# The first stage of a fused cross-attention kernel in a new order: loads in near and far parts, mask sum on ScalarE, all media turned first, mixing and splits interleaved with keys and maxima

## The reference

```
# layer 0, per batch
q  = layernorm(x) @ Wq / 8;   k, v = split(media @ Wkv)        # 16 heads of 64
sim = where(mask, q @ k.T, lowest float)                       # (16, 256, 1601)
x  = x + tanh(attn_gate) * (softmax(sim) @ v) @ Wo
x  = x + tanh(ff_gate) * gelu(layernorm(x) @ W1) @ W2
# layer 1, per batch
mem = media @ W_mem.T;  ctx = softmax(x @ mem.T / 16) @ mem
x = x + sigmoid([x, ctx] @ W_gate.T + b_gate) * ctx;  out = rmsnorm(x) * norm_w
```

## Time and profile before

| what | us |
|---|---|
| device time, median of 3 runs | 901.36 (900.8 to 902.85) |
| span of the profiled execution, first to last instruction | 897.9 |
| busy in that span: PE, DVE, ACT, POOL | 849.0, 592.1, 460.7, 397.7 |

### The profile page before, as it was taken

How to read it: one execution, slowest core, us unless ns; L and a number is a source line. 1 busy time by engine, 2 the same in 40 slices (tenths; PEclk the granted TensorE clock), 3 DMA queues, 4 the chain that set the end, 5 groups by cost and what they waited for, 6 DMA issues and landing times.

```text
span 897.9 us, 18267 instructions
## 1 busy us (share of the span) xinstructions
PE 849.0 (95%) x7811; PEld 709.2 (79%) x7811; DVE 592.1 (66%) x955; ACT 460.7 (51%) x724; POOL 397.7 (44%) x180
## 2 busy tenths in 40 slices
PE   3789999999999999999999999999999999999987
PEld 2478878888878888888888888888887778888775
DVE  6666688867848888677588886756787612043363
ACT  3465555656635556575356665735554441234352
POOL 2155555555645556566256565663566550000000
PEclk9699999999999999999999999999999999999999
DMA  9000001000000010000000000000001500001100
GB/s 273 24 1 1 1 1 38 1 2 1 2 1 1 1 38 2 1 1 2 1 2 1 1 1 2 1 2 1 1 2 39 166 1 0 1 1 37 38 24 23
DMA packets 19842, 16.67 MB, mean 19 GB/s; under 512 B 930, under 2 KB 18739, under 8 KB 19763
## 3 DMA queue, kind: packets, MB, share of 16 engines
q1 hardware_dynamic: 19474, 15.25, 5.8%
q10 hardware_dynamic: 288, 0.27, 0.1%
HBM read 14.46 MB, written 1.05 MB: 17 GB/s over the span
## 4 chain that ended last, share of the span: by engine, by line
PE 78%; DVE 12%; ACT 5%; issue 2%; POOL 1%; DMA 1%; POOLq 0%; DVEq 0%
PE psum L1239 21%; PE psum L1253 16%; PE psum L338 14%; PE psum L1204 6%; PE psum L1162 3%; PE psum L1268 3%; PE psum L1017 3%; PE psum L1031 3%; PE psum L1104 3%; DVE mx L871 2%; DVE k_lo L860 2%; DVE ot L901 1%; PE psum L1259 1%; POOL acc L435 1%; ACT k_hi L591 1%
## 5 line engine op out<-in xcount | busy, mean ns | idle before, releaser
L435 POOL TENSOR_TENSOR acc<-acc,ring 128x1024 f32<-128x1024 f32 x128 | 306.6, 2396 | 18.7 <-POOL acc L435 0.5
L871 DVE TENSOR_REDUCE mx<-psum 128x2 f32<-128x800 f32 (+2 forms) x256 | 245.5, 990 | 88.4 <-PE psum L1204 80.6
L614 ACT ACTIVATE ring<-psum 128x1024 f32<-128x1024 f32 x192 | 196.8, 1026 | 67.6 <-PE psum L1239 61.0
L430 POOL TENSOR_TENSOR acc<-ring 128x1024 f32<-128x1024 f32 x32 | 76.6, 2394 | 283.9 <-ACT ring L614 283.9
L1253 PE MATMUL psum<-ring,v 128*64 128x256 f32 (+1 forms) x1664 | 186.7, 381 | 1.7
L1253 PEld LDWEIGHTS psum<-ring,v 128*64 128x64 f32 (+1 forms) x1664 | 116.7, 137 | 61.0 <-DVE k_lo L860 3.8
L1239 PE MATMUL psum<-nm,maskrow 64*128 64x256 f32 (+1 forms) x832 | 124.1, 294 | 0.6 <-ACT ring L614 0.6
L1239 PE MATMUL psum<-q_hi,k_hi 64*128 64x256 f32 (+1 forms) x832 | 117.3, 278 | 0.0
L1239 PE MATMUL psum<-q_lo,k_hi 64*128 64x256 f32 (+1 forms) x832 | 117.0, 277 | 0.0
L1239 PE MATMUL psum<-q_hi,k_lo 64*128 64x256 f32 (+1 forms) x832 | 117.0, 277 | 0.0
L608 ACT COPY od<-psum 128x512 f32<-128x512 f32 x32 | 18.8, 587 | 172.3 <-PE psum L1259 172.3
(11 more groups left out here) (151 smaller groups left out, 1371.2 us busy)
## 6 DMA issues: line engine op xcount, KB each, us to landing
nat<-in_ctx_dram SPq DMA_DIRECT2D x8, 768.0 KB
w<-in_L_xattn_W_dram SPq DMA_DIRECT2D x2, 1024.0 KB, 8.1
ring<-in_L_xattn_Wkv_dram SPq DMA_DIRECT2D x2, 512.0 KB, 10.1
wq<-in_L_xattn_Wq_dram SPq DMA_DIRECT2D x1, 1024.0 KB, 10.2
wo<-in_L_xattn_Wo_dram SPq DMA_DIRECT2D x1, 1024.0 KB, 11.1
out_dram<-t_res SPq DMA_DIRECT2D x8, 128.0 KB, 1.8
mask<-in_mask_BxS_bk_dram SPq DMA_DIRECT2D x4, 200.1 KB, 6.9
xs<-in_x_dram SPq DMA_DIRECT2D x3, 256.0 KB, 6.7
```

Source lines behind the costliest of these rows:

```text
L430: nc.gpsimd.tensor_tensor(acc[:, :, :, :], ring[:, 0, :, :, :], ring[:, 1, :, :, :], ALU.add)\
L435: nc.gpsimd.tensor_tensor(acc[:, :, :, :], acc[:, :, :, :], ring[:, g, :, :, :], ALU.add)\
L614: nc.scalar.activation(ring[:, g, :, :, :], score_set[m % 2].rearrange("p (h i q) -> p h i q", h=2, i=2), ACT.Exp).then_inc(S["p_ready"], 1)
L871: nc.vector.tensor_reduce(mx[:, t, :, c], pair[:, :, 0:min(c1, KEYS) - c0], axis=AX.X, op=ALU.max).then_inc(S["m_max"], 1)
```

## The change

It does these things. The media of batch 0 load in two parts (six tiles, then the rest), and Wk, Wq and Wv in a near part (the first 256 columns, `NEAR`) and a far part. The mask sum of every batch is an ACT activation with accumulation instead of a DVE reduction; DVE's scalars (B) wait for it, and the inverted mask (J) is an item of its own, placed later. The masked copy T reads the mask itself instead of the inverted mask. In the first stage Z comes ahead of all T, four units of T ahead of W, and G.4 (ACT's q_hi too) ahead of the splits; the low part of q is a new item Q. The items P and K of one chunk alternate, and K.8.2 and the splits alternate with the first maxima. I.1.0, I.1.1, V.4.5 and V.4.6 move back, V.4.6 behind the first scores. POOL now makes the high part of Wv as well, splits the near parts when they are there, and the far parts after the last mt_lo; the first exponential waits for the far parts.

```
...
+FULL_EXTRAS = {2: "G.3 Q.3", 3: "T.1.0 T.1.1 T.1.2", 4: "T.1.3 T.1.4", 5: "W.1", 6: "G.4 Q.4", 7: "G.5 Q.5", 9: "O.0 H.0 G.6 Q.6"}
+COLUMN_EXTRAS = {2: "B.1 J.1", 3: "X.1", 4: "Z.1 C.1 Y.1.0 Y.1.1 Y.1.2 Y.1.3", 5: "P.1.0 P.1.1 P.1.2 P.1.3", 7: "I.1.0 I.1.1"}
...
     ahead = [i for i in body if i[1] >= AHEAD[i[0]]]
-    early = items("""X.1 B.1 I.1.0 T.1.0 T.1.1 Z.1 T.1.2 W.1 T.1.3 T.1.4 C.1 Y.1.0 P.1.0 Y.1.1 P.1.1 Y.1.2 P.1.2 Y.1.3 P.1.3 G.4
-                     K.8.0 K.8.1 K.8.2 K.8.3 M.8.0 M.8.1 L.8.0 M.8.2 M.8.3 L.8.1 L.8.2 L.8.3 I.1.1 V.4.0 M.8.4 V.4.1 M.8.5 V.4.2
-                     M.8.6 V.4.3 M.8.7 V.4.4 N.8 V.4.5 V.4.6 K.9.0 L.9.0 K.9.1 L.9.1 R.8 K.9.2 L.9.2 K.9.3 L.9.3""")
-    behind_scores = items("G.5")
+    early = items("""X.1 B.1 Z.1 T.1.0 T.1.1 T.1.2 T.1.3 W.1 T.1.4 G.4 J.1 C.1 Y.1.0 Y.1.1 P.1.0 K.8.0 Y.1.2 P.1.1 K.8.1 Y.1.3 P.1.2
+                     K.8.2 P.1.3 L.8.0 M.8.0 M.8.1 K.8.3 L.8.1 Q.4 M.8.2 M.8.3 I.1.0 V.4.0 V.4.1 L.8.2 M.8.4 M.8.5 V.4.2 V.4.3
+                     L.8.3 M.8.6 M.8.7 I.1.1 V.4.4 K.9.0 K.9.1 N.8 R.8 L.9.0 L.9.1 K.9.2 L.9.2 K.9.3 L.9.3 V.4.5 S.8.0""")
+    behind_scores = items("V.4.6 G.5 Q.5")
...
     TUNITS = -(-KT // TURN)
+    NEAR = 4 * HD
...
 
-    FIRST_KEYS = (3, 1, 0, 2)
+    FIRST_BANKS = dict(zip(items("T.1.0 T.1.1 T.1.2 T.1.3 W.1 T.1.4 G.4 K.8.0 K.8.1 K.8.2 K.8.3 V.4.5"),
+                           (0, 1, 2, 3, 1, 0, 2, 3, 0, 1, 3, 0)))
 
     def bank_of(order, item):
-        return FIRST_KEYS[item[2]] if order is FIRST and item[:2] == ("K", PAIRS) else BANK[item]
+        return FIRST_BANKS.get(item, BANK[item]) if order is FIRST else BANK[item]
...
             sp.dma_start(mask8[:, 0, :], media_mask[0:1, :].broadcast_to([P, KEYS])).then_inc(S["mask0_in"], 16)
-            sp.dma_start(nat0[:, 0:KT - 1, :], media_full[0, :, :, :]).then_inc(S["media_in"], 16)
+            sp.dma_start(nat0[:, 0:2 * TURN, :], media_full[0, :, 0:2 * TURN, :]).then_inc(S["media0_in"], 16)
+            sp.dma_start(nat0[:, 2 * TURN:KT - 1, :], media_full[0, :, 2 * TURN:KT - 1, :]).then_inc(S["media_in"], 16)
             sp.dma_start(nat0[0:TAIL, KT - 1, :], media_tail[0, :, :]).then_inc(S["media_in"], 16)
-            sp.dma_start(raw_kv[:, 0:INNER], Wkv[:, 0:INNER]).then_inc(S["wk_in"], 16)
-            sp.dma_start(wq[:, :, :], Wq.rearrange("(t p) n -> p t n", p=P)).then_inc(S["wq_in"], 16)
-            sp.dma_start(raw_kv[:, INNER:2 * INNER], Wkv[:, INNER:2 * INNER]).then_inc(S["wv_in"], 16)
+            wq_v = Wq.rearrange("(t p) n -> p t n", p=P)
+            for part, w in enumerate((slice(0, NEAR), slice(NEAR, INNER))):
+                sp.dma_start(raw_kv[:, w], Wkv[:, w]).then_inc(S["wk_in", part], 16)
+                sp.dma_start(wq[:, :, w], wq_v[:, :, w]).then_inc(S["wq_in", part], 16)
+                sp.dma_start(raw_kv[:, INNER:2 * INNER][:, w], Wkv[:, INNER:2 * INNER][:, w]).then_inc(S["wv_in", part], 16)
...
             reciprocal_root(0, "rstd_ready")
-            pool.wait_ge(S["wk_in"], 16)
-            nc.gpsimd.tensor_copy(wk_hi[:, :], raw_kv[:, 0:INNER]).then_inc(S["kv_hi"], 1)
-            for i, (lo, hi) in enumerate(((wk_lo, wk_hi), (wv_lo, wv_hi))):
-                pool.wait_ge(S["kv_hi"], i + 1)
-                nc.gpsimd.tensor_tensor(lo[:, :], raw_kv[:, i * INNER:(i + 1) * INNER], hi[:, :].bitcast(F32),
-                                        ALU.subtract).then_inc(S["kv_split"], 1)
+            for n, w in enumerate((slice(0, NEAR), slice(NEAR, INNER))):
+                if n:
+                    pool.wait_ge(S["mt_lo"], NCH)
+                for i, (name, lo, hi) in enumerate((("wk_in", wk_lo, wk_hi), ("wv_in", wv_lo, wv_hi))):
+                    raw = raw_kv[:, i * INNER:(i + 1) * INNER]
+                    pool.wait_ge(S[name, n], 16)
+                    nc.gpsimd.tensor_copy(hi[:, w], raw[:, w]).then_inc(S["kv_hi"], 1)
+                    pool.wait_ge(S["kv_hi"], 2 * n + i + 1)
+                    nc.gpsimd.tensor_tensor(lo[:, w], raw[:, w], hi[:, w].bitcast(F32), ALU.subtract)\
+                        .then_inc(S["kv_split"], 1)
...
                     kind, n = item[0], item[1]
-                    if order is FIRST and item == ("I", 1, 1):
-                        act.wait_ge(S["wv_in"], 16)
-                        nc.scalar.copy(wv_hi[:, :], raw_kv[:, INNER:2 * INNER]).then_inc(S["kv_hi"], 1)
                     if kind in USES_BANK:
                         bank = aux[bank_of(order, item)]
-                    if kind == "P":
+                    if kind == "B":
+                        if order is FIRST:
+                            act.wait_ge(S["mask0_in"], 16)
+                        upto(act, "qs_ready", b, n)
+                        nc.scalar.activation(unread[:, :], mask8[:, b + 1, :], ACT.Copy, accum_out=msum[:, 0:1])\
+                            .then_inc(S["mask_summed"], 1)
+                    elif kind == "P":
...
                         upto(act, "s_full", b, 2 * (m + 1))
+                        if order is FIRST and item == ("S", PAIRS, 0):
+                            act.wait_ge(S["kv_split"], 4)
...
 
-                        if order is FIRST:
-                            dve.wait_ge(S["mask0_in"], 16)
-                        step(nc.vector.reduce_sum(msum[:, 0:1], mask8[:, b + 1, :], axis=AX.X))
+                        upto(dve, "mask_summed", b, n + 1)
                         nc.vector.tensor_scalar(msum[:, 1:2], msum[:, 0:1], 0.5, None, ALU.is_le)
                         step(nc.vector.tensor_scalar(msum[:, 2:3], msum[:, 0:1], 1.0, None, ALU.max))
                         nc.vector.tensor_scalar(qs[:, :], msum[:, 1:2], -Q_SCALE, Q_SCALE, ALU.mult, ALU.add)\
                             .then_inc(S["qs_ready"], 1)
                         step(nc.vector.reciprocal(msum[:, 3:4], msum[:, 2:3]))
+                    elif kind == "J":
                         nc.vector.tensor_scalar(inv8[:, :], mask8[:, b + 1, :], msum[:, 1:2], 0.5, ALU.max, ALU.is_lt)\
                             .then_inc(S["inv_ready"], 1)
                     elif kind == "T":
                         c0, c1 = turned(item[2])
                         upto(dve, "t_full", b, n * TUNITS + item[2] + 1)
-                        upto(dve, "inv_ready", b, n + 1)
-                        nc.vector.scalar_tensor_tensor(mt[:, c0:c1], inv8[:, c0:c1], 0.5, bank[:, 0:c1 - c0],
-                                                       ALU.is_lt, ALU.mult).then_inc(S["mt_in"], 1)
+                        nc.vector.scalar_tensor_tensor(mt[:, c0:c1], mask8[:, b + 1, c0:c1], msum[:, 1:2],
+                                                       bank[:, 0:c1 - c0], ALU.max, ALU.mult).then_inc(S["mt_in"], 1)
                     elif kind == "C":
                         upto(dve, "part_in", b, (n + 1) * TUNITS)
                         step(nc.vector.reduce_sum(msum[:, 4:5], part[:, :], axis=AX.X))
+                        upto(dve, "inv_ready", b, n + 1)
...
                                                 ALU.subtract).then_inc(S["mt_lo"], 1)
-                    elif kind == "G":
+                    elif kind == "Q":
                         upto(dve, "q_hi", b, n + 1)
+                        bank = aux[bank_of(order, ("G", n))]
...
                     if kind == "T":
-                        if item[2] == 0:
+                        if order is FIRST and item[2] == 0:
+                            pe.wait_ge(S["media0_in"], 16)
+                        elif item[2] == 2 * (order is FIRST):
...
                     elif kind == "G":
-                        if order is FIRST and n == PAIRS // 2:
-                            pe.wait_ge(S["wq_in"], 16)
+                        if order is FIRST and n < PAIRS // 2 + 2:
+                            pe.wait_ge(S["wq_in", n - PAIRS // 2], 16)
...
                             pe.wait_ge(S["kv_split"], 1)
+                        if order is FIRST and item == ("K", PAIRS + 2, 0):
+                            pe.wait_ge(S["kv_split"], 4)
...
```

More of the change, by code:

```diff
@@ L34 @@
          "F": PAIRS, "V": PAIRS // 2, "G": PAIRS // 2, "O": 1, "H": 1, "T": 1, "B": 1, "C": 1, "Y": 1, "P": 1, "X": 1, "Z": 1,
-         "W": 1, "I": 1}
-FULL_EXTRAS = {2: "G.3", 3: "T.1.0 T.1.1 T.1.2", 4: "T.1.3 T.1.4", 5: "W.1", 6: "G.4", 7: "G.5", 9: "O.0 H.0 G.6"}
-COLUMN_EXTRAS = {2: "B.1", 3: "X.1", 4: "Z.1 C.1 Y.1.0 Y.1.1 Y.1.2 Y.1.3", 5: "P.1.0 P.1.1 P.1.2 P.1.3", 7: "I.1.0 I.1.1"}
+         "W": 1, "I": 1, "J": 1, "Q": PAIRS // 2}
+FULL_EXTRAS = {2: "G.3 Q.3", 3: "T.1.0 T.1.1 T.1.2", 4: "T.1.3 T.1.4", 5: "W.1", 6: "G.4 Q.4", 7: "G.5 Q.5", 9: "O.0 H.0 G.6 Q.6"}
+COLUMN_EXTRAS = {2: "B.1 J.1", 3: "X.1", 4: "Z.1 C.1 Y.1.0 Y.1.1 Y.1.2 Y.1.3", 5: "P.1.0 P.1.1 P.1.2 P.1.3", 7: "I.1.0 I.1.1"}
 LAST_EXTRAS = {("A", 2): "s.0", ("A", 3): "s.1", ("A", 4): "s.2", ("A", 5): "n.0 n.1 n.2", ("F", 5): "z.0 z.1",
@@ L291, in cross_attention_kernel @@
```

(7 more changed lines are left out.)

## The result

The changed kernel takes 895.88 us (median of 4 runs, 894.79 to 896.77) against 902.11 (900.8 to 903.49) for the kernel before, run beside it: a ratio of 0.9934, 95% interval 0.9917 to 0.995. So it is faster by 6.2 us, where 3.6 were forecast; the time lies in the range. The profiled execution of after took 896.53 us, with a span of 894.7, which is 3.2 less than the span before.

A forecast was written before the change was run, and what follows sets the result against it. PE was taken as the bound from the start of G.5 on. First-stage steps put that start at 55.05 instead of 58.64; 3.6 off the 897.9 span is 894.3, plus 3.46 gives 897.8 us, range 893.8 to 900.8.

The forecast's parts named there:

- G.4: Eight matmuls with Wq on PE in the first stage: start at 16.15, no weight wait, 3.73 us at half clock.
- rounds: Key matmuls, ACT's copy and split, DVE's low part as a closed chain, three times: 2.4 + 3.1 + 3.1 = 8.6 us.
- N.8: Two short DVE instructions behind the first eight maxima: end at 42.0 us, where before it was 44.7.
- the wait ahead of M.9.2: First scores on PE: with S.8.0 ahead of M.9.0, M.9.2 waits for a maximum, about 1.0 us lost.
- the mark: Start of G.5, behind which both orders run the same items: 55.05 us, 3.6 ahead of 58.64.
- The median of the runs is 3.46 above that span: Last step, from profiled span to median time: 3.46 us added to 894.3, giving 897.8.
- The two instructions of z: DVE in the first stage: 0.40 us each, plus 0.2 of a possible 0 to 0.6 beside POOL's near subtraction.
- ACT's sum: Mask sum moved from DVE to ACT: taken as 1.7 us, ending at 10.9, gaining nothing by itself (+0.1).
- More won by an early full clock: Rival: PE at full clock earlier in the first stage, 4.3 us together, most likely about 895; chance 30%.
- Given back by a late Wq: Rival: Wq's near part lands late and delays G.4; with 3 us the time is 900.8; chance 12%.
- Slower by half clock into the scores: Rival: PE stays at half clock into the first scores, 5.2 us and part of the scores: 903; chance 10%.
- That split and key don't overlap: Rival: splitting and keys, named as interleaved, are in series on ACT; already counted in the sum, no separate chance.

The follow-up runs named there:

- c_after: The changed kernel, unaltered, timed and profiled once more: 895.4 us, ratio 0.9921 to the kernel before.
- second pair: New profiles of the unaltered kernel before and changed kernel, each run once more: spans of 900.3 and 893.5 us, medians 902.63 and 895.4.
- e_loads: Changed kernel with the old weight order, both parts of Wk, then of Wq, then of Wv: 896.27 us, ratio 0.9936 to the kernel before.
- e_mask_dve: Changed kernel with the mask sum back as DVE's reduction in all four batches: 895.95 us, ratio 0.9929 to the kernel before.
- e_s_behind: The kernel of e_all with S.8.0 put back behind M.9.0, as in the kernel before: 886.37 us, ratio 0.9826.
- e_fill_after: Changed kernel with unread transposes added in PE's gaps ahead of W.1, G.4 and the first three keys: 893.53 us, ratio 0.9905.
- e_fill_before2: Kernel before with the added transposes of e_fill_before and 22 more ahead of M.8.3 and V.4.0: 898.43 us, ratio 0.9961.
- e_split_first: Changed kernel with each split one place ahead of the key before it: 890.62 us, ratio 0.987 to the kernel before.
- e_q_behind: Changed kernel with G.4 placed behind the first split in the list: 892.91 us, ratio 0.9893 to the kernel before.
- e_all: Changed kernel with all four splits ahead of G.4, first maxima behind the second key, low part of q earlier: 887.0 us, ratio 0.9831.
- e_fill_before: Kernel before with unread transposes added in PE's gaps ahead of W.1, T.1.3 and the four first keys: 900.54 us, ratio 0.9983.
- e_all_fill: The kernel of e_all with unread transposes added in PE's gaps ahead of W.1 and G.4: 888.07 us, ratio 0.984.

## Why the prediction was right, and what it mis-sized

**The timetable held.** Its steps against the trace of after: z ready 12.45 and 12.27; G.4 16.15 and 16.07, at 3.75 us; rounds 2.4 + 3.1 + 3.1 and 3.05 each (in c_after the first took 2.5, the later two 3.05); the last mt_lo 30.3 and 30.7; N.8 42.0 and 42.3; S.8.0 45.1 and 45.37; the wait ahead of M.9.2 1.0 and 0.94; G.5 55.05 and 55.32. Behind the mark nothing changed, as forecast: 839.3 to 839.8 us in all four profiles.

**Where the 3.3 us of the first pair come from.** The splits won nothing: the maxima begin when they did before (31.13 for 31.18), and all four keys were done by then before, only three after. From the first maximum to the end of N.8 it is 11.2 us instead of 13.5. In the timelines of PE and DVE before, PE waits 2.54 us for the low parts of the keys ahead of V.4.0, and DVE then waits for PE's maxima; K.9.0 comes behind N.8:

```profile
36.37 0.58 PE L338 MATMUL psum<-wv_hi,mt_hi 128*128 128x256 f32 x1 [2.54 <-DVE k_lo L860]
...
45.17 0.35 PE L338 MATMUL psum<-mt_hi,wk_hi 128*128 128x402 f32 x1
```

```profile
38.72 0.99 DVE L871 TENSOR_REDUCE mx<-psum 128x2 f32<-128x800 f32 x1 [1.92 <-PE psum L1204]
...
40.67 0.99 DVE L871 TENSOR_REDUCE mx<-psum 128x2 f32<-128x800 f32 x1 [0.96 <-PE psum L1204]
```

In the new order V.4.0 and V.4.1 stand ahead of L.8.2, V.4.0 begins at 33.70 without a wait, and of DVE's waits 0.90 and 0.25 are left. That is 2.4 of the 3.3 us. Between N.8 and the first scores 1.9 more are won (4.98 us before, 3.06 after), with K.9.0 at 40.82, ahead of N.8; from the first scores to G.5 1.0 is given back, by the wait ahead of M.9.2. This is read from the timelines: no run undoes these places of the order one by one.

**The step that was mis-sized is the last one, from span to median.** "The median of the runs is 3.46 above that span" took the whole distance as the time around the span. That is only 1.8 us; the other 1.7 were a short execution of before, in which the clock rose early. Worked through: 897.8, plus 0.4 for the span (894.7 for 894.3), less 1.7, is 896.5, the profiled execution of after; its median is 0.65 lower still. The same mistake makes the gain: 3.2 us between the first two profiles, 6.2 to 7.0 between the medians. Of the second pair's 6.7 us at the mark, 1.9 more than in the first come from before, whose clock rose later, and 1.5 from after, which began earlier and had its first key at full clock. The runs of the changed kernel lie within 0.6 us in c_after, but within 2.0 in the first timing, so that its work is less exposed to a late rise is not shown. The median of 895.88 lies just below the forecast's own 896.0 to 899.3, among the times that the prediction gave to an early full clock: that it stayed in the range owes something to the width of the range, not to this last step.

**Small terms.** The two instructions of z took 1.14 us, not 0.80, beside POOL's near subtraction (11.30 to 12.12). The Trainium skill, "SBUF — State Buffer", section "SBUF: two separate sides", says that GpSimd and some VectorE instructions lock a port pair that they share; the trace agrees with it, and the price was 0.3 us of the 0 to 0.6 that the prediction allowed. In e_loads, where POOL's subtraction ended 0.28 us after z had begun, z took 0.76. ACT's sum was 1.54 and 0.19 for the read-out, for the 1.7 taken; e_mask_dve shows no difference from moving it. The place of S.8.0, counted as 1.0 lost, is worth some 0.2 by e_s_behind, since PE waits elsewhere without it.

**The rivals.** More won by an early full clock: the median is near that case's 895, but not by that way; G.4 and the later rounds were at half clock, and e_fill_after, which gave G.4 and the first three keys full clock but not the values, found 1.9 us, so the case's 4.3 were not tried whole. In the kernel before, the clock alone is worth more than half of what the change won: e_fill_before2 took off 3.9 us. Given back by a late Wq: out, G.4 waited for zt in after and in e_loads. Slower by half clock into the scores: out; the value products of after take 0.28 us from 38.28 on, half-clock ones 0.42. The Trainium skill, "TensorE: Matmul & The Clock Gate", section "HAM oscillation — how this bites in real kernels", warns that gaps in the matmul stream put the clock back to its low level. The fall came (c_after reads 0.50 behind the gaps between keys), but 903 was not what followed: with the values unbroken the clock was back by 38 us. That split and key don't overlap was in the sum, and e_split_first, e_q_behind and e_all price it: 4.8, 2.5 and together 8.1 to 8.4 us, more than the change won itself.

## What to carry to other kernels

Where several engines walk one list, place an item by the queue of each engine that has a part in it: here copies on ACT that could wait stood ahead of a split that all waited for, and another order of the same items was worth more than the whole change. By the timelines here, values and keys that need none of the pending results are worth moving into the wait of an engine that the others wait for. Put a profile beside the time of its own execution, and take a second one, before a span is turned into a median. A gap on PE is priced by what runs behind it at half clock, and filling some gaps of a stretch can leave the price where it was.

## What was not expected

- With PE busy in every window, the rise of the clock came at about 40 us in one execution of before and at about 44 in another.
- Fills that left one gap only moved the fall: to 28 us in e_fill_after, to 32 to 34 in e_fill_before. In e_all_fill it came behind a gap of 1.20 us.
- In the profile of after the granted clock reads 1.00 in the windows where key matmuls took 0.54 instead of 0.35 us (the first row below is such a window); durations decide there, not the column. So it is with G.4: in the kernel before the column reads 1.00 while it took 3.73 us (second row), so the half clock that the prediction gives it rests on its duration alone. In e_all the same eight matmuls take 3.75 with the column at 0.50 (third row), and 1.97 in e_fill_after.

```profile
24.00:26.00 2.00, 1.22 (x3) 0.83 (x3) 1.12 (x2) 0.02 (x1) 0.00 (x0) 1.00 0.14 34
...
20.00:22.00 2.00, 2.00 (x7) 1.55 (x6) 1.12 (x4) 0.85 (x4) 0.00 (x0) 1.00 0.69 199
...
16.00:18.00 2.00, 2.00 (x5) 1.64 (x6) 1.82 (x5) 0.84 (x3) 0.00 (x0) 0.50 1.09 345
```
